# Eight expert-output pairs held before the last stage, and that stage in seven parts instead of six

## The reference

```python
def reference(x, src, dst, edge_weight, ...):
    # 12500 nodes x 256 features
    x = x + gnn(layernorm(x), src, dst, edge_weight, W, b)   # 200000 weighted edges, segment sum, linear layer
    x = x + ffn(layernorm(x), ...)                           # below
    return x

def ffn(x):
    h = (x @ W_gat).reshape(M, HEADS, NUM_EXPERTS)           # 4 heads, 4 experts
    e = leaky_relu(a_src[src] + a_dst[dst])                  # 131072 edges and a loop for each node
    ee = exp(e - segment_max(e, dst)[dst])
    alpha = ee / (segment_sum(ee, dst)[dst] + 1e-16)
    agg = segment_sum(h[src] * alpha[:, :, None], dst) + b_gat
    scores = layernorm(agg, ln_gamma, ln_beta).reshape(M, HEADS, NUM_EXPERTS).mean(1)
    topk_s, topk_i = top_k(scores, 2)
    w = softmax(topk_s)
    out = 0
    for ei in range(NUM_EXPERTS):
        g = where(topk_i == ei, w, 0).sum(-1)
        out = out + g[..., None] * (gelu(x @ W1[ei] + b1[ei]) @ W2[ei] + b2[ei])
    return out
```

## Time and profile before

| | us |
|---|---|
| median of 3 runs | 3662.67 (3661.21 to 3663.2) |
| the profiled execution, its own time | 3665.02 |
| its span | 3663.2 |
| start of `combine` in it | about 3487 |
| TensorE busy over the span | 2973.1 (81%) |
| VectorE | 2040.8 (56%) |
| ScalarE | 819.5 (22%) |
| GpSimd | 2708.5 (74%) |

### The profile page before, as it was taken

One profiled execution on the slowest core, in us unless ns is written; L12 is line 12 of the kernel. 1 busy time (PEld: TensorE's weight loads), 2 busy tenths in 40 slices (PEclk: granted clock), 3 DMA queues, 4 the chain that ended last, 5 costly groups with the idle time before them and its releaser, 6 DMA issues. The chain is left out here.

```text
span 3663.2 us, 60252 instructions
## 1 busy us (share of the span) xinstructions
PE 2973.1 (81%) x13893; PEld 2429.7 (66%) x13894; DVE 2040.8 (56%) x6854; ACT 819.5 (22%) x2321; POOL 2708.5 (74%) x2817
## 2 busy tenths in 40 slices
PE   1475665666866889978889799999999999999748
PEld 1354444554645666656666688888888888888637
DVE  8777668787787676563443322443443344342567
ACT  6300000000110111212222222233232323232247
POOL 6677777777777777777777777777777777777673
PEclk6787877787877999999999899999999999999879
DMA  9643333333333444444444222242222222232279
GB/s 348 195 123 105 107 110 112 110 115 112 116 115 112 120 123 123 124 121 124 128 131 127 62 76 54 54 119 57 73 54 73 57 73 56 71 73 60 60 285 385
DMA packets 276697, 425.17 MB, mean 116 GB/s; under 512 B 59304, under 2 KB 210355, under 8 KB 275507
## 3 DMA queue, kind: packets, MB, share of 16 engines
q0 software_dynamic: 114208, 217.09, 23.4%
q1 hardware_dynamic: 64319, 114.73, 8.5%
q10 hardware_dynamic: 98004, 91.50, 7.7%
HBM read 317.12 MB, written 105.98 MB: 115 GB/s over the span
## 5 line engine op out<-in xcount | busy, mean ns | idle before, releaser
L673 POOL DMA_INDIRECT rows<-feats,src_t x1500 | 1453.7, 969 | 464.2 <-issue 444.7
L1202 POOL DMA_INDIRECT got<-row_dram,src_sorted x1024 | 990.8, 968 | 312.2 <-issue 312.2
L836 PE MATMUL node_sums<-rows,ys_ahead 128*128 x3904 | 989.2, 407 | 232.7 <-SPq L657 116.9
L836 PEld LDWEIGHTS node_sums<-rows,ys_ahead 128*128 128x128 f32 x3904 | 761.7, 202 | 428.7 <-issue 314.6
L1285 PE MATMUL d_hidden<-d_yt,w 128*128 128x256 f32 x3136 | 710.4, 380 | 0.8 <-DVE d_yt L1371 0.8
L1296 PE MATMUL d_expert<-w,hid 128*128 128x256 f32 x3136 | 708.7, 379 | 0.0
L1296 PEld LDWEIGHTS d_expert<-w,hid 128*128 128x128 f32 x3136 | 595.8, 190 | 81.0
L1285 PEld LDWEIGHTS d_hidden<-d_yt,w 128*128 128x128 f32 x3136 | 593.1, 190 | 80.1 <-DVE d_yt L1371 1.2
L1348 DVE TENSOR_TENSOR yo<-d_expert,x_and_b 128x512 f32<-128x512 f32 x196 | 135.6, 692 | 837.6 <-PE d_expert L1296 830.1
L895 DVE TENSOR_SCALAR ys_ahead<-iota,rel,ew_t 128x128 f32<-128x128 f32 x1952 | 557.2, 363 | 65.1 <-DVE rel L891 2.0
L1229 ACT ACTIVATE hid<-d_hidden,b1c 128x256 f32<-128x256 f32 x784 | 324.5, 472 | 979.6 <-PE d_hidden L1285 789.1
(11 more groups left out here) (305 smaller groups left out, 2277.7 us busy)
## 6 DMA issues: line engine op xcount, KB each, us to landing
y_dram<-yo ACTq DMA_DIRECT2D x196, 256.0 KB, 2.2
ys<-y_dram SPq DMA_DIRECT2D x36, 1024.0 KB, 9.2
rows<-feats,src_t POOLq DMA_INDIRECT x1500
got<-row_dram,src_sorted POOLq DMA_INDIRECT x1024, 2.4
ys_ahead<-y_dram SPq DMA_DIRECT2D x13, 1024.0 KB, 9.2
x_dram<-edge_plan ACTq DMA_DIRECT2D x98, 128.0 KB
d_x<-x_dram ACTq DMA_DIRECT2D x49, 256.0 KB, 3.0
ys_ahead<-in_x ACTq DMA_DIRECT2D x97, 128.0 KB
```

What stands on the lines that cost most here:

```text
L673: pool.indirect_dma_start(rows[:, g % RING, j, :], None, feats, bass.IndirectOffsetOnAxis(ap=m.src_t[:, g * GT + j:g * GT + j + 1], axis=0 ...
L836: t = pe.matmul(psA[:, ds(((code >> 1) & 1) * 512, FEAT)], hot[:, r, j, :], rows[:, ds((code >> 2) & (RING - 1), 1), j, :], start=False, s ...
L1202: pool.indirect_dma_start(got[:, k, j, 0:ROWF], None, m.row_dram, bass.IndirectOffsetOnAxis(ap=m.src_sorted[:, BEGIN[b] + j:BEGIN[b] + j + ...
```

## The change

Four more pairs of expert outputs are loaded before `combine`. After the store of the seventh block of states SyncE waits for the last expert matmul, for all stores of expert outputs and for the rows of the eighth block, and then loads pairs 4 to 7 into the buffers of w1 and w2, two in each. So w1, w2, b1c and b2r are kept to the end, and `combine` allocates eight slots instead of twelve; there are still 16 in all. `combine` loads the three small vectors first and then slots 8 to 15.

`PART` has seven parts of 8, 10, 14, 18, 20, 18 and 10 tiles. The first has no pair on VectorE; the others have each fifth, third, third, fourth, third and second. So 16 pairs are on VectorE and 33 on TensorE. The TensorE pairs are, by parts, 4 (pairs 0 to 3), 4 (5 to 8), 4 (10, 11, 13, 14), 6, 7, 6 and 2; before they were 3, 6, 7, 7, 7 and 2. The code that orders ScalarE is the same. Two semaphores of the first stage are merged into others there.

```diff
+LATE = 4
...
-            return layers.enter_context(nc.sbuf_tensor(name, shape, F32))
...
-        m.w1 = weights("w1", [P, HALVES, EXPERTS, HID])
-        m.w2 = weights("w2", [P, FB, EXPERTS, FEAT])
+        m.w1 = keep("w1", [P, HALVES, EXPERTS, HID])
+        m.w2 = keep("w2", [P, FB, EXPERTS, FEAT])
...
+        m.y_slots = [m.ys_ahead[:, k] for k in range(AHEAD)]
+        for t in (m.w1, m.w2):
+            m.y_slots += pairs_of(t[:].rearrange("p a b c -> p (a b c)"))
...
-        layers.close()
...
-                v.reciprocal(rstd[:, k, :], rstd[:, k, :]).then_inc(s_rcp, 1)
-                v.wait_ge(s_rcp, n + 1)
+                c.done(v.reciprocal(rstd[:, k, :], rstd[:, k, :]))
...
+        def landed(eng, b):
+
+            for q in range(4):
+                if in_quarter(b, q):
+                    eng.wait_ge(s_got[b % NBUF][q], 16 * sum(in_quarter(a, q) for a in range(b % NBUF, b + 1, NBUF)))
...
+                if b == len(BLOCK_PAIR) - 1:
+                    sp.wait_ge(s_l2, PAIRS * EXPERTS)
+                    for e in range(EXPERTS):
+                        sp.wait_ge(s_st[e], 16 * PAIRS)
+                    landed(sp, BLOCKS - 1)
+                    for k in range(AHEAD, AHEAD + LATE):
+                        load_pair(sp, m, k, k, m.y_slots[k])
...
-        PART = [0, 10, 28, 48, 68, 88, T]
+        PART = [0, 8, 18, 32, 50, 70, 88, T]
+        EVERY = [PAIRS, 5, 3, 3, 4, 3, 2]
         PARTS = len(PART) - 1
         BY_VECTOR = [i for n in range(PARTS) for i in range(PART[n] // 2, PART[n + 1] // 2)
-                     if (i - PART[n] // 2) % (4 if n < PARTS - 1 else 2) == 0]
+                     if n > 0 and (i - PART[n] // 2) % EVERY[n] == 0]
...
-        ys_more = sb("ys", [P, SLOTS - AHEAD, 2, EXPERTS, FEAT])
+        ys_more = sb("ys", [P, SLOTS - AHEAD - LATE, 2, EXPERTS, FEAT])
...
-            for k in range(AHEAD, SLOTS // 2):
-                load_pair(sp, m, k, k, y_of(k))
             for n, a in enumerate((b_gat, gamma, beta)):
                 sp.dma_start(vec[:, n, :], a.rearrange("(o c) -> o c", o=1).to_broadcast([P, HE])).then_inc(s_c, 16)
-            for k in range(SLOTS // 2, SLOTS):
+            for k in range(AHEAD + LATE, SLOTS):
                 load_pair(sp, m, k, k, y_of(k))
```

More of the change, by code:

```diff
@@ L128, in build @@
         m.s_store = [sem(f"tile_stored{k}") for k in range(SLOTS)]
-        layers = top.enter_context(ExitStack())
-        def weights(name, shape):
-            return layers.enter_context(nc.sbuf_tensor(name, shape, F32))
         m.plan = keep("edge_plan", [P, 3 * ECOLS])
@@ L136, in build @@
         m.ys_ahead = keep("ys_ahead", [P, AHEAD, 2, EXPERTS, FEAT])
-        m.w1 = weights("w1", [P, HALVES, EXPERTS, HID])
-        m.w2 = weights("w2", [P, FB, EXPERTS, FEAT])
-        m.b1c = weights("b1c", [P, EXPERTS, FB])
-        m.b2r = weights("b2r", [P, EXPERTS, FEAT])
+        m.w1 = keep("w1", [P, HALVES, EXPERTS, HID])
+        m.w2 = keep("w2", [P, FB, EXPERTS, FEAT])
+        m.b1c = keep("b1c", [P, EXPERTS, FB])
+        m.b2r = keep("b2r", [P, EXPERTS, FEAT])
         with ExitStack() as part1:
@@ L162, in build, with pairs_of @@
             weighted_sums(nc, sem, feats, edge_index, x, W, b, W_gat, att_src, att_dst, W1, b1, W2, b2, m)
+        def pairs_of(flat):
+            n = 2 * EXPERTS * FEAT
+            return [flat[:, a:a + n].rearrange("p (t e f) -> p t e f", e=EXPERTS, f=FEAT)
+                    for a in range(0, flat.shape[1] - n + 1, n)]
+        m.y_slots = [m.ys_ahead[:, k] for k in range(AHEAD)]
+        for t in (m.w1, m.w2):
+            m.y_slots += pairs_of(t[:].rearrange("p a b c -> p (a b c)"))
+        assert len(m.y_slots) == AHEAD + LATE
         attention_and_experts(nc, sem, m)
-        layers.close()
         combine(nc, sem, b_gat, gamma, beta, out, m)
@@ L238, in layernorm_and_plan @@
         s_const = sem("a_const")
-        s_raw0 = sem("a_raw_cleared")
+        s_raw0 = sem("a_inputs_cleared")
         s_raw = [sem("a_src_loaded"), sem("a_dst_loaded"), sem("a_weight_loaded")]
@@ L242, in layernorm_and_plan @@
         s_scale = sem("a_scale")
-        s_clear = sem("a_x_cleared")
         s_var, s_std, s_norm = sem("a_var"), sem("a_std"), sem("a_norm")
-        s_rcp = sem("a_reciprocal")
         s_v, s_t, s_ev = sem("a_statistics"), sem("a_turned"), sem("a_turn_read")
@@ L277, in load @@
                     sp.dma_start(xin[k][:, 0:CH - 1, :], x_tiles[:, n * CH:FULL_TILES, :]).then_inc(s_xin[k], 16)
-                    sp.wait_ge(s_clear, 1)
+                    sp.wait_ge(s_raw0, 4)
                     sp.dma_start(xlast[0:LAST_ROWS, :], x[FULL_TILES * P:NODES, :]).then_inc(s_xin[k], 16)
@@ L313, in _ @@
             pool.memset(m.eps[:], LN_EPS).then_inc(s_const, 1)
-            pool.memset(xlast[:], 0.0).then_inc(s_clear, 1)
+            pool.memset(xlast[:], 0.0).then_inc(s_raw0, 1)
             pool.iota(m.iota[:], pattern=[[1, P]], base=0, channel_multiplier=0,
@@ L1187, in _ @@
                     for k in range(AHEAD):
-                        load_pair(sp, m, k, k, m.ys_ahead[:, k])
+                        load_pair(sp, m, k, k, m.y_slots[k])
[5 more added lines that the diff above has]
+                    for k in range(AHEAD, AHEAD + LATE):
+                        load_pair(sp, m, k, k, m.y_slots[k])
         @block.gpsimd
@@ L1388, in maxima @@
                 j = slice(BEGIN[b], BEGIN[b + 1])
-                for q in range(4):
-                    if in_quarter(b, q):
-                        v.wait_ge(s_got[b % NBUF][q], 16 * sum(in_quarter(a, q) for a in range(b % NBUF, b + 1, NBUF)))
+                landed(v, b)
                 c.done(v.tensor_scalar(limit[:, 0:n], m.seg_keep[:, j], 2 * BIG, -BIG, ALU.mult, ALU.add))
@@ L1577, in y_of @@
             k = i % SLOTS
-            return m.ys_ahead[:, k] if k < AHEAD else ys_more[:, k - AHEAD]
+            return m.y_slots[k] if k < AHEAD + LATE else ys_more[:, k - AHEAD - LATE]
         def out_of(i):
```

## The result

The changed kernel takes 3682.01 us (median of 5 runs, 3681.35 to 3683.21) where the kernel before takes 3662.67 (5 runs, 3661.16 to 3663.20). The ratio is 1.0053, with an interval of 1.0041 to 1.0064: slower by 19.3 us. Its profiled execution took 3682.24 us, with a span of 3680.5.

What follows compares the result with a forecast made beforehand. Bound: a loop of gates, ScalarE's order and TensorE. Six turns in 156.1 us for five in 131.7, starting 3.1 earlier, with an end 2.2 shorter, give 19.1 more: 3662.67 + 19.1 = 3681.8 us, range 3673 to 3689.

Steps and rivals of the forecast that it cites:

- The loop: In combine, gates, ScalarE's in-order exponential and TensorE pairs pace each other; a part costs about 23 to 28 us.
- The rest of the gates after the exponential: From the exponential's end to the gates' end in combine: 8.4 to 11.6 us a part, hardly less when small.
- The landing: Wait for the last gather before combine's first gates, taken as 7.1 us from the earlier trace.
- The ways to the exponential: From one part's gates to the next exponential's end in combine: 15.6 us first, then 16.1, with 14.1 after part 4.
- The first pair after an idle stretch: TensorE's first pair at the fallen clock takes 5.6 us where others take 3.45, counted three times within the 16.1.
- The end: After the last gates, pairs 45 and 47: 2.45 for diagonals, 0.15, then 3.69 + 3.45, 9.8 us in all.
- a start that has moved: First row of combine expected near 3487 as now; a moved start would favour late loads holding up the states store.
- the small edits in the first stage: Reordered vector loads and merged semaphores wait for the same work in the same order: 0 us.
- transfers bind: Rival: transfers bound combine, so four fewer pairs to load save 10.2 us, giving 3652; chance 0.06.
- small parts overlap better: Rival: small parts' gates get out during ScalarE's waits for TensorE, so gains and losses cancel at 3663; chance 0.06.
- the late loads hold up the last store of states: Rival: loads queued before combine delay that store; at half rate 8 us more, 3690; chance 0.04.
- The tables: Two more ScalarE table loads in combine; at the skill's 2.66 us a switch, up to 2.7 us more if uncovered.

Runs made afterwards that it cites:

- The run with the functions early: Changed kernel with ScalarE asked for the next part's exponential, square root and other exponential after 1, 2, 3 TensorE pairs instead of 4, 5, 6: 3667.13 us.
- the run with the parts alone: Changed kernel with slots 4 to 7 filled at the start of combine as before the change, seven parts and 16 VectorE pairs kept: 3685.11 us.
- the kernel with the late loads alone: Changed kernel with the six parts and VectorE pairs of before, keeping pairs 4 to 7 loaded before combine: 3661.68 us, 0.9997 of the kernel before.
- the two runs with the busy matmuls: Changed kernel plus 14, 17 and 19 unread matmuls ahead of pairs 5, 10 and 17: 6107.15 and 6097.69 us, 1.0045 and 1.0044 of the kernel before.
- the kernel with more TensorE pairs: Changed kernel with VectorE pairs 4, 9, 12 and 15 given to TensorE (37 pairs there): 6102.93 us, 1.0048 of the kernel before.

## Why the prediction was right

It said 3681.8 and 19.1 us more; it is 3682.0 and 19.3. The mechanism held. That the number fits to 0.2 us is in part luck: inside `combine` the sum was 2.2 us short, and the traces differ by more than that outside it (both below). Step by step, with each event counted from the first gather of `combine` (3487.91 before, on which the prediction's times rest, and 3483.71 after):

| | predicted | measured |
|---|---|---|
| gates of part 0 | 24.8 | 23.6 |
| part 1 | 48.8 | 48.3 |
| part 2 | 74.5 | 73.8 |
| part 3 | 101.4 | 101.5 |
| part 4 | 129.1 | 129.8 |
| part 5 | 154.5 | 155.1 |
| part 6 | 180.9 | 181.4 |
| end of TensorE's work | 190.7 | 192.9 |

**The loop holds.** The rest of the gates after the exponential came to 9.55, 10.8, 11.6, 11.2 and 10.3 us in parts 2 to 6, each within 0.15 of the term used. The three idle stretches of 8 to 11 us are there. The run with the functions early shows that it is ScalarE's order that makes them, and the run with the parts alone that they are the loss.

**The landing was put too long.** The first gates were to wait 7.1 us for the last gather, as in the earlier trace rows; it took 6.0. The row had twelve 1 MB loads on the queue, not the eight that stand there now: with eight it is 6.04 here and 5.55 in the kernel with the late loads alone, with twelve 6.94 to 8.12.

**The ways to the exponential were put a little short**: 16.4, 15.95, 16.9 and 16.7 us for 15.6, 16.1, 16.1 and 16.1. The first pair after an idle stretch was put at 5.6 us, from one row of before; from its first matmul to its copy it takes 6.0, 5.6, 6.5 and 6.3 in the four cold starts. The prediction took one stretch for all three. Its readings were also a little low: from 3541.45 to 3547.15 are 5.7 us, not 5.6, and the way worked out from the rows is 16.2, not 16.1.

**The end was put short**: 9.8 us from the last gates to TensorE's end, where it took 11.5. The prediction gave the last two pairs the 3.45 us of a warm engine (one at the full clock). The window of TensorE there, kernel after (columns as in the earlier trace rows, whose second and third window have a clock of 1.00):

```profile
3665.00:3670.00 5.00, 3.12 (x11) 2.26 (x10) 4.84 (x15) 4.76 (x16) 0.00 (x0) 0.82 0.20 67
```

The two pairs took 8.85 us (in the chain above) at a granted clock of 0.82, behind gaps of 1.2 and 1.9 us, where a warm pair of pairs takes 7.14. This is a term that was overlooked, of 1.7 us.

**Two deviations partly cancel.** In the two profiled executions `combine` is 21.5 us longer (196.8 for 175.3, first gather to the span's end), 2.4 more than forecast, and starts 4.2 us earlier. The prediction had the start near 3487 as now, and called a start that has moved a sign against it; it had a later one in mind. The kernel before with its first part on TensorE has the same code as the kernel before up to `combine`, and the chain of its trace starts it as early as the changed kernel's:

```profile
3483.64 0.97 POOL edge_plan L1626
```

The shift is old by then. The first expert matmul, at the start of `attention_and_experts`, is at 2074.6 us in the trace of before, at 2070.5 in that other trace of the same code and at 2071.2 with the change. And the gathers of `weighted_sums` took longer in the trace of before. The group of these gathers in its page, and in the page of the other kernel:

```profile
L673 POOL DMA_INDIRECT rows<-feats,src_t x1500 | 1453.7, 969 | 464.2 <-issue 444.7
...
L673 POOL DMA_INDIRECT rows<-feats,src_t x1500 | 1448.4, 966 | 466.3 <-issue 444.3
```

So most of the 4.2 us are scatter between executions. The profiled execution of before was a late one, 2.3 us over its median, as the prediction said. That leaves some 2 us between the 21.5 of the traces and the 19.3 of the medians which no row assigns. The execution with the start at 3483.64 was itself 1.7 us below its median, so a gain of this size from the small edits in the first stage, which the prediction put at 0, is not excluded.

**The rivals.** That transfers bind falls with the late loads alone (10 us of transfer less, 0.9 us gained, and the interval of the ratio holds 1). That small parts overlap better falls with the turns of 24.7 and 25.5 us. That the late loads hold up the last store of states falls with the timeline of SyncE's queue, kernel after:

```profile
3460.47 2.06 SPq L1088 DMA_DIRECT2D w<-y_dram  x4
...
3472.55 0.34 SPq L1190 DMA_DIRECT2D state_dram<-got  x1
```

The loads start when the rows of the eighth block have landed, and the row of the store ends 12.4 us later; before, too, it ended 12.4 us behind the landing. From there to the first gather of `combine` it is 10.8 us, before 10.9. `combine` starts at 3483.71, as the kernels without late loads do (3483.64 and 3483.77). That they cost nothing was right. That they buy nothing was right with six parts; beside seven, the same parts without them take 3.1 us more by the medians.

**The tables.** The Trainium skill (ScalarE: Activation LUTs, "What ACT_TABLE_LOAD costs") puts a switch at 2.66 us with its drain. The trace has less. In the small parts both loads of 1.28 us lie in time that ScalarE spends waiting for VectorE, and none of it reached the path. Where ScalarE does not wait, as in the gates of part 4, a copy ends at 3610.71, the load follows, and the next function starts at 3612.03: 1.32 us from one instruction to the next for the whole switch, not 2.66.

## What to carry to other kernels

In a loop that goes through several engines, count the turns before the work: here a turn cost 24.7 and 26.4 us for 10 tiles and 28.3 for 20, because the request of the next turn stood behind a fixed number of pairs in an in-order queue. Cutting such a stage finer starts it earlier once (the first gates came 4.3 us earlier within the stage) and pays a turn for each cut, unless each piece leaves work to run under the next turn; moving the request forward in the queue took 14.9 of the 19.3 us back (medians of two groups), until the next engine in the loop became the late one. A transfer share of 1.03 with nobody waiting for a load is not a bound, and taking 4 of 45 loads out of the stage gained nothing by itself.

## What the runs showed of the hardware

- With the same code up to there, the last stage started at 3483.64 us in one execution and at 3487.91 in another, on chips whose medians for the kernel agree (3662.57 and 3662.67). 4.1 us of it were there at the first expert matmul, behind 1500 gathers that took 966 ns each in the one and 969 in the other. That is a fifth of what was to be measured, and has to be taken out before two traces are set side by side.
- The landing of a small gather moved with the large loads beside it: 6.04 us with eight loads of 1 MB on the queue and 8.12 with twelve; for a gather 2.5 us later in the stage, 5.55 with eight and 7.07 and 6.94 with twelve.
- The granted clock fell behind gaps of 1.22 and 1.89 us between pairs at the end of the kernel, to 0.82, and two pairs took 8.85 us. In one of the two runs with the busy matmuls the same two pairs behind the same gaps took 7.16, in the other 8.85. The same pattern of work can meet either clock, 1.7 us apart.
- The same kernel took 3663 us on one chip and 6069 to 6144 us on others. The page of the kernel with more TensorE pairs, from such a chip, has this group, where the last columns are the idle time and what ended most of it:

```profile
L1217 POOL DMA_INDIRECT got<-row_dram,src_sorted x1024 | 1006.1, 983 | 1306.5 <-DMA state_dram<-got 989.3
```

And the same line of the page of the kernel after, from the usual chip:

```profile
L1217 POOL DMA_INDIRECT got<-row_dram,src_sorted x1024 | 989.6, 966 | 312.1 <-issue 312.1
```

GpSimd's gathers themselves last as long (983 and 966 ns), but it waits 989 us for stores of states to HBM that cost it no wait on the usual chip, and TensorE stands for 37.10 and 45.49 us in the chain of `combine` there. The 989 us are less than half of the 2413 us between the medians; the rest is not assigned. Why the waits are there is open; no run here was made for it. What it teaches is that an experiment is worth little away from the chip of its comparison: eight of the twelve answered only what steps inside one trace can answer.
